# Square roots for the recurrence's rows in three parts inside attention, rows normalized in place and stored in groups, turned blocks copied out on two engines

## The chip, the cores and the metric

The kernel runs on one core of one Trainium2 chip. The metric is the device time of one launch in microseconds (us). Three runs of the kernel before took 3347.38, 3348.98 and 3350.77 us, with a median of 3348.98 us. The core has five engines that run their own instruction queues side by side: TensorE (PE) for matrix products and transposes, VectorE (DVE), ScalarE (ACT), GpSimd (POOL) and SyncE (SP). They meet only through semaphores. Transfers between memory and the core's buffers run on 16 DMA engines. They are issued from the queues of SP, ACT or POOL.

## The reference

Two layers work on `x` (32 batches of 100 rows of 256 numbers) with a context of 361 rows per batch:

```python
x = x + tanh(g_xattn[0]) * L0_xattn(layernorm(x), ctx, ctx, Wq, bq, Wk, bk, Wv, bv, Wo, bo)
x = x + tanh(g_ffn[0])   * L0_ffn(layernorm(x), gru_w_ih, gru_w_hh, expr_w, ctx_w, ctx_b, gate_w, up_w, down_w, ...)
x = x + tanh(g_xattn[1]) * L1_xattn(ctx, layernorm(x))
x = x + tanh(g_ffn[1])   * L1_ffn(layernorm(x), router_w, w1, b1, w2, b2)
```

`L0_xattn` is attention with 16 heads. `L0_ffn` is a GRU of 100 steps that routes rows to experts. `L1_xattn` is an alignment by dynamic programming, and `L1_ffn` a mixture with a capacity. `layernorm(x)` is `(x - mean) / sqrt(var + 1e-5)` over each row. The change touches what lies between attention and the GRU: the normalization of the rows that attention gives.

## The kernel before

The kernel is a chain of stages. Each stage is a block: all five engines run their part, and at its end they meet. Each engine reports to POOL that it has drained (the gather), and POOL releases all of them into the next stage. The stages that matter here are these.

**Attention** (`attention`, about 30 to 750 us of the span) handles one batch in a turn. The 32 turns are software pipelined over the engines: `pipelined` (L218 to L227) writes out turn 0 and turn 31 and puts turns 1 to 30 in a loop of two turns each. In a turn the engines walk over the 16 heads. PE computes the scores of four heads at a time (L573), DVE takes the maxima (L456), ACT the exponentials (L380), PE transposes the results (L581), and DVE and ACT copy the transposed results of even and odd heads out of PSUM (L505, L390). The four score banks are refilled only when the exponentials of the four heads before are done. The output of batch b is projected and added to its row during turn b+1 (L470, L476), its mean and variance go into `mean_var` (L477 to L488), and POOL stores its rows to memory (`store`, L351). At the end POOL waits until all these stores have landed (the wait on `stored`) before it drains.

**Normalized rows out** (`normalized_rows_out`, L123 to L201) is the next stage, about 756 to 786 us. ACT issues the loads of `wc`, `cb` and `gate`, and POOL that of `wih` (3 MB, for the GRU). Then DVE adds the epsilon for all 32 batches at once, ACT takes the square root, and DVE the reciprocal. For every batch DVE normalizes the rows into one of 8 buffers `h` (L163), SP stores this buffer to `h_store` (L144), PE transposes its two halves into one of 8 PSUM banks (L176), and ACT copies the two halves into `hT` and sums each row on the way (L197). DVE may refill a buffer only when its store has landed and its transposes are done. At the end PE multiplies the sums by `wc` (L182), and DVE makes the first state of the GRU from it (L166).

**The GRU** (`gru`) starts at about 786 us. POOL copies its first inputs from `hT`, and PE needs `wih` and `whh`.

The order on each engine is written out by hand. No scheduler moves instructions. An ACT function that needs another table than the one loaded gets an `ACT_TABLE_LOAD` ahead of it. The compiler puts it in.

## Time and profile before

| | us |
|---|---|
| median of three runs | 3348.98 |
| the profiled execution | 3356.15 |
| its span, first to last instruction | 3354.5 |
| attention ends on DVE (mean and variance of batch 31 kept) | 750.55 |
| next stage released | 755.8 |
| GRU released | 785.8 |

| engine | busy us | share |
|---|---|---|
| PE | 2969.9 | 89% |
| DVE | 1424.3 | 42% |
| ACT | 958.9 | 29% |
| POOL | 815.3 | 24% |

Times in the rows below are counted from the start of the span. A row of the timeline that stands for several instructions gives the start of the first, the time until the end of the last and their number. Since an engine overlaps the end of one instruction with the start of the next, the spacing of starts is what one more instruction costs.

### The profile page before, as it was taken

The numbers are of one execution on the slowest core, as the hardware profiler recorded it, in microseconds if no ns is written. First come the engines' busy times: TensorE is split into PE (matmuls) and PEld (weight loads), VectorE is DVE, ScalarE is ACT, GpSimd is POOL, SyncE is SP. The second block draws the span as 40 slices with busy tenths as digits, with TensorE's granted clock in tenths as the row PEclk, the third lists the DMA queues.
The fourth block names the chain that finished last, engine by engine and source line by source line (L and its number), as shares of the span: only waits on it lengthen the run. The fifth ranks groups of instructions, "written<-read, shape, count | busy, mean of one in ns | idle before, by whom it ended". The sixth has DMA issues, their size and how long they took to land. (4 is left out here: it accounts for less than half of the span.)

```text
span 3354.5 us, 72380 instructions
## 1 busy us (share of the span) xinstructions
PE 2969.9 (89%) x27712; PEld 1662.2 (50%) x27713; DVE 1424.3 (42%) x3167; ACT 958.9 (29%) x2643; POOL 815.3 (24%) x771
## 2 busy tenths in 40 slices
PE   5999999988999999999999999999999976008698
PEld 3666666653444444444444444458666644007454
DVE  4666666652222233333323333345222246985311
ACT  2555555543111111111111111122122236472111
POOL 1111001100222222232222222233444422004243
PEclk9999999987999999999999999999999988558699
DMA  6000000003000000000000000041222253005143
GB/s 225 24 21 20 21 23 23 23 11 128 23 16 23 17 23 17 23 17 17 22 17 23 17 23 17 23 176 53 43 45 45 45 148 119 0 0 198 46 115 72
DMA packets 81216, 163.02 MB, mean 49 GB/s; under 512 B 12056, under 2 KB 54936, under 8 KB 76408
## 3 DMA queue, kind: packets, MB, share of 16 engines
q1 hardware_dynamic: 55848, 102.34, 9.7%
q0 software_dynamic: 21504, 40.67, 5.5%
q10 hardware_dynamic: 3664, 17.04, 1.4%
q8 instruction: 162, 2.65, 0.3%
q14 instruction: 38, 0.31, 0.0%
HBM read 119.63 MB, written 40.37 MB: 48 GB/s over the span
## 5 line engine op out<-in xcount | busy, mean ns | idle before, releaser
L926 PE MATMUL gru_ps_rz<-whh,scratch 128*32 128x512 f32 x6400 | 707.4, 594 | 0.0
L734 POOL TENSOR_TENSOR scratch<-scratch 128x1024 f32<-128x1024 f32 (+3 forms) x246 | 369.6, 1527 | 818.5 <-DVE stat L748 657.6
L926 PEld LDWEIGHTS gru_ps_rz<-whh,scratch 128*32 128x32 f32 x6400 | 197.7, 110 | 452.1 <-issue 452.1
L931 PE MATMUL gru_ps_n<-whh,scratch 128*32 128x256 f32 x6400 | 363.6, 379 | 0.0
L855 DVE TENSOR_TENSOR scratch<-scratch,state 128x256 f32<-128x256 f32 x100 | 50.8, 508 | 661.1 <-ACT scratch L884 661.1
L931 PEld LDWEIGHTS gru_ps_n<-whh,scratch 128*32 128x32 f32 x6400 | 207.9, 110 | 180.1 <-issue 59.8
L380 ACT ACTIVATE att_probs<-att_score,att_neg_max 100x361 f32<-100x361 f32 x512 | 260.6, 568 | 122.2 <-DVE att_neg_max L456 122.1
L581 PEld LDWEIGHTS att_turned<-ident,att_probs 100*121 100x121 f32 x1536 | 210.3, 185 | 140.3 <-issue 105.9
L581 PE MATMUL att_turned<-ident,att_probs 100*121 100x100 f32 x1536 | 267.3, 287 | 11.8 <-ACT att_probs L380 5.0
L456 DVE TENSOR_REDUCE att_neg_max<-att_score 100x1 f32<-100x361 f32 x512 | 250.1, 525 | 56.0 <-PE att_score L573 56.0
L884 ACT ACTIVATE scratch<-gru_ps_rz 128x512 f32<-128x512 f32 x100 | 59.7, 597 | 720.3 <-PE gru_ps_rz L926 720.3
L903 PE MATMUL gru_ps_rz<-wih,scratch 128*32 128x512 f32 x1600 | 191.5, 596 | 2.2 <-POOL scratch L823 2.2
L2219 PE MATMUL e_ps_g<-align_reach,ident 32*121 32x101 f32 x64 | 10.9, 326 | 196.8 <-DVE align_reach L2031 195.3
L748 DVE TENSOR_REDUCE stat<-scratch 128x2048 f32 (+3 forms) x96 | 181.1, 1886 | 0.0
L505 DVE COPY att_probsT<-att_turned 121x300 f32<-121x300 f32 x256 | 119.0, 465 | 134.3 <-PE att_turned L581 134.1
L887 ACT ACTIVATE scratch<-scratch 128x256 f32<-128x256 f32 x100 | 41.7, 417 | 349.0 <-DVE scratch L859 349.0
L390 ACT COPY att_probsT<-att_turned 121x300 f32<-121x300 f32 x256 | 103.5, 404 | 131.9 <-PE att_turned L581 131.9
L857 DVE TENSOR_TENSOR scratch<-scratch,gru_ps_n 128x256 f32<-128x256 f32 x100 | 42.1, 421 | 231.7 <-PE gru_ps_n L931 231.7
L573 PE MATMUL att_score<-att_kT,att_qT 32*100 32x361 f32 x1024 | 112.3, 508 | 16.1 <-ACT att_probs L380 15.4
L356 POOL TENSOR_TENSOR att_qT<-att_q_all,att_head_mask 128x400 f32<-128x400 f32 x32 | 27.3, 853 | 379.8 <-DVE att_q_all L444 379.7
L1470 DVE COPY mix_room<-mix_ps_m 128x512 f32<-128x512 f32 x57 | 39.4, 691 | 187.7 <-PE mix_ps_m L1559 187.7
L1147 POOL DMA_INDIRECT x<-mix_room,mix_rows_listed x57 | 90.4, 1586 | 92.1 <-ACT mix_room L1205 87.6
(377 smaller groups left out, 4385.2 us busy)
## 6 DMA issues: line engine op xcount, KB each, us to landing
table<-in_w SPq DMA_DIRECT2D x16, 1024.0 KB, 7.0
states<-state SPq DMA_DIRECT2D x100, 128.0 KB
scratch<-states SPq DMA_DIRECT2D x25, 512.0 KB, 3.6
whh<-in_whhT POOLq DMA_DIRECT2D x8, 1536.0 KB, 17.3
att_c_in<-in_ctxT SPq DMA_DIRECT2D x32, 363.0 KB, 3.0
dist_ctx<-in_ctxT SPq DMA_DIRECT2D x32, 363.0 KB, 5.5
align_ctx<-in_ctx_rows SPq DMA_DIRECT2D x32, 363.0 KB
whh<-in_guT ACTq DMA_DIRECT2D x8, 1024.0 KB, 12.1
```

The costliest lines, as they stand in the source:

```text
L380: nc.scalar.activation(probs[h % KEPT][:, 0:KV], score[h % BANKS][0:S, 0:KV], ACT.Exp, bias=neg_max[:, h % KEPT:h % KEPT + 1], scale=-1.0) ...
L390: nc.scalar.copy(probsT[h // 4 % 2][:, h % 4, :], turned[1][0:KC, 0:3 * S]).then_inc(odd_ready, 1)
L456: nc.vector.tensor_reduce(neg_max[:, h % KEPT:h % KEPT + 1], score[h % BANKS][0:S, 0:KV], AX.X, ALU.min).then_inc(max_ready, 1)
L505: nc.vector.tensor_copy(probsT[h // 4 % 2][:, h % 4, :], turned[0][0:KC, 0:3 * S]).then_inc(even_ready, 1)
L573: nc.tensor.matmul(score[r][0:S, 0:KV], qT[u][strip, half, g, :], kT[u][strip, g, 0:KV], start=True, stop=True).then_inc(s_psum, 1)
L581: done = nc.tensor.transpose(turned[h % 2][0:KC, m * S:(m + 1) * S], probs[h % KEPT][:, m * KC:(m + 1) * KC], ident[0:S, 0:S])
L734: done = nc.gpsimd.tensor_tensor(last.prod[:, row:row + rows, :], a, b, ALU.mult)
L748: nc.vector.tensor_reduce(stat[:, bass.ds(it, 1), at:at + rows].rearrange("p a n -> p (a n)"), last.prod[:, 0:rows, :], AX.X, ALU.add).the ...
L903: nc.tensor.matmul(ps_rz[quarter(q), :], xt[u][:, k, j, :], rz_columns(wih, k, q), start=(k == 0), stop=False)
L926: last = nc.tensor.matmul(ps_rz[quarter(q), :], stateT[c % 2][:, quarter(c // 2)], rz_columns(whh, c, q), start=False, stop=(c == GC - 1))
L931: last = nc.tensor.matmul(ps_n[quarter(q), 0:GQ], stateT[c % 2][:, quarter(c // 2)], n_columns(whh, c, q), start=(c == 0), stop=(c == GC - 1))
L1147: nc.gpsimd.indirect_dma_start(x2, bass.IndirectOffsetOnAxis(ap=rows_listed[:, n:n + 1], axis=0), y[u], None, compute_op=ALU.add).then_inc ...
```

## The change

The roots move into attention. The statistics of batches 0 to 23 are complete when turn 25 runs. In turn 25 DVE adds the epsilon for these 24, ACT takes their root between two attention functions, and in turn 26 DVE inverts them. From turn 26 on, DVE normalizes four of these batches a turn, in place in `rows`, after heads 2, 5, 8 and 11. SP stores them in three groups of eight batches, 800 KB each. After the last turn come the epsilon, root, reciprocal and normalization of batches 24 to 30, around the output of batch 31. Batch 31 itself gets its root in the next stage. For this, the turns from 25 to 31 are written out on ACT and DVE (`pipelined_to`), while PE and POOL keep their loop.

In the next stage PE transposes straight from `rows`, with no normalization ahead of it except for batch 31. Of every 8 batches ACT copies out 5, with its sums, and DVE 3, each with a reduction for the sums and a copy for both halves. The last group of eight batches goes out as one store of 800 KB from SP. SP also issues the loads of `wc`, `cb` and `gate`, which ACT issued before. POOL no longer waits for its stores at the end of attention. DVE does before it writes `rows` in place.

```diff
-            v.tensor_scalar(rstd[:], mean_var[:, :, 1], LN_EPS, None, ALU.add).then_inc(eps_added, 1)
+            v.tensor_scalar(rstd[:, LAST:B], mean_var[:, LAST:B, 1], LN_EPS, None, ALU.add).then_inc(eps_added, 1)
             dve.wait_ge(root_ready, 1)
-            v.reciprocal(rstd[:], rstd[:]).then_inc(scaled, 1)
-            dve.wait_ge(scaled, 1)
+            v.reciprocal(rstd[:, LAST:B], rstd[:, LAST:B]).then_inc(inverted, 1)
             for b in range(B):
-                if b >= RING:
-                    dve.wait_ge(h_stored[b % RING], 16 * (b // RING))
-                    dve.wait_ge(h_turned, b - RING + 1)
-                v.tensor_scalar(h[b % RING][:], rows[:, b, :], mean_var[:, b, 0:1], rstd[:, b:b + 1], ALU.subtract, ALU.mult).then_inc(h_ready, 1)
+                if b == BANKS:
+                    dve.wait_ge(inverted, 1)
+                    for u in range(2):
+                        dve.wait_ge(x1_stored[u], 16 * (B // 2))
+                    v.tensor_scalar(rows[:, LAST, :], rows[:, LAST, :], mean_var[:, LAST, 0:1], rstd[:, LAST:B],
+                                    ALU.subtract, ALU.mult).then_inc(last_ready, 1)
+                if not BY_ACT[b % BANKS]:
+                    dve.wait_ge(h_turned, b + 1)
+                    halves = turned[b % BANKS][:, 0:KT * S].rearrange("p (k s) -> p k s", k=KT)
+                    v.tensor_reduce(x_sum[:, :, b], halves, AX.X, ALU.add).then_inc(sums_done, 1)
+                    v.tensor_copy(hT[:, :, :, b], halves).then_inc(dve_copied, 1)
...
         @block.sync
         def _(sp):
-            for b in range(B):
-                sp.wait_ge(h_ready, b + 1)
-                sp.dma_start(h_rows[b], h[b % RING][:]).then_inc(h_stored[b % RING], 16)
-            for u in range(RING):
-                sp.wait_ge(h_stored[u], 16 * (B // RING))
+            sp.dma_start(wc[:], wcT).then_inc(wc_in, 16)
+            for q in range(4):
+                sp.dma_start(cb[32 * q:32 * q + 32, :], ctx_b[q * GQ:(q + 1) * GQ].partition_broadcast(32)).then_inc(cb_in, 16)
+            sp.dma_start(gate[:, :], g_ffn.partition_broadcast(P)).then_inc(gate_in, 16)
+            sp.wait_ge(last_ready, 1)
+            sp.dma_start(h_rows[:, EARLY:B, :], rows[:, EARLY:B, :]).then_inc(h_stored, 16)
+            sp.wait_ge(h_stored, 16 * (EARLY // 8 + 1))
...
+def pipelined_to(engine, looped, count, turn_of):
+
+    turn_of(0, 0, True, False)
+    with engine.Fori(1, looped // 2 + 1) as i:
+        turn_of(2 * i - 1, 1, False, False)
+        turn_of(2 * i, 0, False, False)
+    for b in range(looped + 1, count):
+        turn_of(b, b % 2, False, b == count - 1)
...
+                    if isinstance(b, int) and b == EARLY + 1 and h == ROOTS:
+                        roots(0, EARLY, 1)
...
-            pipelined(act, B, turn_of)
+            pipelined_to(act, EARLY, B, turn_of)
+            roots(EARLY, B - 1, 2)
             att_out(B - 1)
             attnT_out(B - 1)
...
+                    if isinstance(b, int) and b >= EARLY + 2 and h % 3 == 2 and h < 12 and 4 * (b - EARLY - 2) + h // 3 < EARLY:
+                        normalize_output(4 * (b - EARLY - 2) + h // 3, 1, 16 * (EARLY // 2 + 1), 16 * (EARLY // 2))
...
             pipelined(pool, B, turn_of)
-            store(B - 1)
-            pool.wait_ge(stored, 16 * B)
-            pool.wait_ge(cleared_rows, 16)
+            store(B - 1, 1)
```

Here `EARLY` is 24, `ROOTS` is 6 and `BY_ACT` is `(True, True, False, True, False, True, True, False)`.

ACT in turn 25, from the exponentials ahead of head 6 on. Before, the turn is in the loop (line 378 and 227 rows are register work of the loop, 380 exponentials, 390 the copies of odd heads, 394 and 402 copies of two small transposed blocks):

```order
L380 ACTIVATE att_probs<-att_score,att_neg_max 100x361 [waits att_t_psum,att_max_ready]
L390 COPY att_probsT<-att_turned 121x300 [waits att_o_psum,att_t_psum]
L393 REGISTER_ALU
L394 COPY att_xnT<-att_misc 128x200 [waits att_xnT_psum]
L402 COPY att_attnT<-att_misc 128x200 [waits att_attnT_psum]
L390 COPY att_probsT<-att_turned 121x300 [waits att_o_psum,att_t_psum]
L378 REGISTER_ALU
L227 REGISTER_ALU [waits att_max_ready]
L380 ACTIVATE att_probs<-att_score,att_neg_max 100x361 [waits att_t_psum]
```

The same place in the changed kernel, where 413 are the exponentials, 423 the copies of odd heads, and 440 the root:

```order
L413 ACTIVATE att_probs<-att_score,att_neg_max 100x361 [waits att_t_psum,att_max_ready] x4
L423 COPY att_probsT<-att_turned 121x300 [waits att_o_psum,att_t_psum]
L427 COPY att_xnT<-att_misc 128x200 [waits att_xnT_psum]
L435 COPY att_attnT<-att_misc 128x200 [waits att_attnT_psum]
L440 ACT_TABLE_LOAD
L440 ACTIVATE rstd_x<-rstd_x 100x24 [waits att_eps_added]
L423 COPY att_probsT<-att_turned 121x300 [waits att_o_psum,att_t_psum]
L413 ACT_TABLE_LOAD [waits att_t_psum]
L413 ACTIVATE att_probs<-att_score,att_neg_max 100x361 [waits att_max_ready]
L413 ACTIVATE att_probs<-att_score,att_neg_max 100x361 [waits att_t_psum,att_max_ready] x3
```

Two table loads and the root have come between the copy of the attention output and the next exponential, with the copy of head 7 between the loads.

DVE in turn 26, from the copy of head 2 on. Before (505 copies, 456 maxima, 462 and 464 the division of the batch before):

```order
L505 COPY att_probsT<-att_turned 121x300 [waits att_o_psum,att_t_psum]
L454 REGISTER_ALU
L227 REGISTER_ALU [waits att_s_psum]
L456 TENSOR_REDUCE att_neg_max<-att_score 100x1 [waits att_p_ready]
L454 REGISTER_ALU
L227 REGISTER_ALU [waits att_s_psum]
L456 TENSOR_REDUCE att_neg_max<-att_score 100x1 [waits att_p_ready]
L454 REGISTER_ALU
L227 REGISTER_ALU [waits att_s_psum]
L456 TENSOR_REDUCE att_neg_max<-att_score 100x1 [waits att_p_ready]
L462 RECIPROCAL att_inverse<-att_misc 100x16 [waits att_back_psum]
L464 TENSOR_TENSOR att_attn<-att_misc,att_inverse 100x256 [waits att_inverse_ready]
```

Now (564 copies, 497 maxima, 546 a normalization in place):

```order
L564 COPY att_probsT<-att_turned 121x300 [waits att_o_psum,att_t_psum]
L497 TENSOR_REDUCE att_neg_max<-att_score 100x1 [waits att_p_ready,att_s_psum]
L546 TENSOR_SCALAR rows_x<-rows_x,mean_var,rstd_x 100x256 [waits x1_stored1,x1_stored0,att_rstd_ready]
L497 TENSOR_REDUCE att_neg_max<-att_score 100x1 [waits att_p_ready,att_s_psum] x2
L503 RECIPROCAL att_inverse<-att_misc 100x16 [waits att_back_psum]
L505 TENSOR_TENSOR att_attn<-att_misc,att_inverse 100x256 [waits att_inverse_ready]
L564 COPY att_probsT<-att_turned 121x300 [waits att_o_psum,att_t_psum]
L497 TENSOR_REDUCE att_neg_max<-att_score 100x1 [waits att_p_ready,att_s_psum]
L546 TENSOR_SCALAR rows_x<-rows_x,mean_var,rstd_x 100x256 [waits x1_stored1,x1_stored0,att_rstd_ready]
```

The first normalization of the turn stands between the first and the second of three maxima. The second stands after the maximum of head 7. The register work of the loop is gone.

SP from the end of attention to the GRU. In the changed kernel it issues three grouped stores in attention, then (from L145 on, the next stage) the loads and the last group:

```order
L365 DMA h_store<-rows_x 100x2048 [waits att_h_ready] x3
L284 UNCONDITIONAL_BRANCH
L145 UNCONDITIONAL_BRANCH [waits barrier_Pool_Activation_PE_DVE_SP_release]
L147 DMA wc<-in_wcT 128x2048
L149 DMA cb<-in_ctx_b 32x256 x4
L150 DMA gate_ffn<-in_g_ffn 128x2
L152 DMA h_store<-rows_x 100x2048 [waits last_h_ready]
L129 UNCONDITIONAL_BRANCH [waits h_stored]
```

Before, SP had only the 32 stores of one batch each in that stage. The loads of `wc`, `cb` and `gate` now stand ahead of the last store in SP's own queue.

## Rows read from the trace of the kernel before

**Rows 1.** The page's busy times of the whole span.

```profile
PE 2969.9 (89%) x27712; PEld 1662.2 (50%) x27713; DVE 1424.3 (42%) x3167; ACT 958.9 (29%) x2643; POOL 815.3 (24%) x771
```

**Rows 2.** Windows: us, busy of PE, PEld, DVE, ACT, POOL, then clock, DMA share, GB/s.

```profile
702.00:724.00 22.00, 21.06 (x221) 15.10 (x219) 14.57 (x38) 13.09 (x31) 2.16 (x3) 1.00 0.02 5
724.00:746.00 22.00, 17.52 (x174) 12.16 (x175) 11.15 (x28) 9.57 (x23) 0.54 (x1) 0.75 0.02 5
766.00:768.00 2.00, 0.00 (x0) 0.00 (x0) 0.00 (x0) 0.00 (x0) 0.00 (x0) 0.50 1.15 412
774.00:776.00 2.00, 2.00 (x10) 1.16 (x8) 1.74 (x6) 2.00 (x21) 0.00 (x0) 0.50 0.68 236
```

**Rows 3.** Queue instructions at attention's end (L253): duration ns min/median/max, start.

```profile
L253 POOLq DRAIN  x1: 3407/3407/3407, 752.2 to 752.2; - x1
L253 SPq EVENT_SEMAPHORE  x1: 17/17/17, 755.8 to 755.8; - x1
```

**Rows 4.** The same at the end of the stage after it (L126).

```profile
L126 POOLq DRAIN  x1: 13105/13105/13105, 756.4 to 756.4; - x1
L126 SPq EVENT_SEMAPHORE  x1: 17/17/17, 785.8 to 785.8; - x1
```

**Rows 5.** Timeline of DVE, 740 to 795 us: start, us, what, idle before.

```profile
750.32 0.23 DVE L488 TENSOR_SCALAR mean_var<-att_mean_var_now 100x2 f32<-100x2 f32 x1
...
760.92 2.67 DVE L163 TENSOR_SCALAR h<-rows_x,mean_var,rstd_h 100x256 f32<-100x256 f32 x8
769.83 5.20 DVE L163 TENSOR_SCALAR h<-rows_x,mean_var,rstd_h 100x256 f32<-100x256 f32 x12 [6.24 <-DMA h_store<-h]
...
791.19 0.29 DVE L849 COPY scratch<-gru_ps_t 128x128 f32<-128x128 f32 x1 [5.82 <-PE gru_ps_t L912]
```

**Rows 6.** Timeline of ACT in the stage, 756 to 782 us.

```profile
758.98 1.28 ACT L193 ACT_TABLE_LOAD   x1 [12.24 <-issue]
760.27 0.23 ACT L193 ACTIVATE rstd_h<-rstd_h 100x32 f32<-100x32 f32 x1
...
770.93 0.35 ACT L197 ACTIVATE hT<-turned 128x100 f32<-128x100 f32 x1 [5.05 <-PE turned L176]
...
781.58 0.71 ACT L197 ACTIVATE hT<-turned 128x100 f32<-128x100 f32 x1
```

**Rows 7.** Timeline of PE in the stage.

```profile
761.39 2.93 PE L176 MATMUL turned<-ident,h 100*128 100x100 f32 x16 [12.57 <-DVE h L163]
```

**Rows 8.** DMA issues, 735 to 800 us: count, KB each, median us to landing.

```profile
wih<-in_wihT POOLq DMA_DIRECT2D x1, 3072.0 KB, 13.0
...
gate_ffn<-in_g_ffn ACTq DMA_DIRECT2D x1, 1.0 KB, 11.6
```

**Rows 9.** Timeline of ACT, turn 30, heads 5 to 10.

```profile
708.71 0.35 ACT L402 COPY att_attnT<-att_misc 128x200 f32<-128x200 f32 x1
709.76 0.41 ACT L390 COPY att_probsT<-att_turned 121x300 f32<-121x300 f32 x1 [0.70 <-PE att_turned L581]
710.06 1.47 ACT L380 ACTIVATE att_probs<-att_score,att_neg_max 100x361 f32<-100x361 f32 x3
```

**Rows 10.** Timeline of PE, turn 30 (first three rows) and turn 31.

```profile
707.33 0.56 PE L581 MATMUL att_turned<-ident,att_probs 100*121 100x100 f32 x3
708.37 0.87 PE L573 MATMUL att_score<-att_kT,att_qT 32*100 32x361 f32 x8 [0.47 <-ACT att_probs L380]
...
710.76 0.55 PE L581 MATMUL att_turned<-ident,att_probs 100*121 100x100 f32 x3
...
731.26 0.56 PE L581 MATMUL att_turned<-ident,att_probs 100*121 100x100 f32 x3 [0.96 <-ACT att_probs L380]
...
734.37 1.54 PE L573 MATMUL att_score<-att_kT,att_qT 32*100 32x361 f32 x8
```

**Rows 11.** Timeline of DVE, turn 30, heads 2 to 4.

```profile
704.58 1.41 DVE L456 TENSOR_REDUCE att_neg_max<-att_score 100x1 f32<-100x361 f32 x3 [0.39 <-PE att_score L573]
...
706.81 0.47 DVE L505 COPY att_probsT<-att_turned 121x300 f32<-121x300 f32 x1 [0.19 <-PE att_turned L581]
```

More of the change, by code:

```diff
@@ L120, in normalize, with normalized_rows_out @@
     return nc.vector.tensor_scalar(out, rows, mean[:, bass.ds(b, 1)], rstd[:, bass.ds(b, 1)], ALU.subtract, ALU.mult)
-def normalized_rows_out(nc, rows, mean_var, h_rows, hT, ident, wih, wihT, wih_in, wcT, ctx_b, state, gate, g_ffn):
-    RING, BANKS = 8, 8
+def normalized_rows_out(nc, rows, mean_var, rstd, x1_stored, h_rows, h_stored, cleared_rows, hT, ident, wih, wihT, wih_in,
+                        wcT, ctx_b, state, gate, g_ffn):
+    BANKS = 8
+    BY_ACT = (True, True, False, True, False, True, True, False)
+    LAST = B - 1
     with ExitStack() as ctx:
-        h = [ctx.enter_context(nc.sbuf_tensor(f"h{u}", [S, DIM], F32)) for u in range(RING)]
-        rstd = ctx.enter_context(nc.sbuf_tensor("rstd_h", [S, B], F32))
         x_sum = ctx.enter_context(nc.sbuf_tensor("x_sum", [P, KT, B], F32))
@@ L150, in _ @@
             pool.dma_start(wih[:], wihT).then_inc(wih_in, 16)
+            pool.wait_ge(cleared_rows, 16)
         @block.vector
@@ L330, in _ @@
             repeat(sp, B // 2, turn_of)
+            for g in range(EARLY // 8):
+                sp.wait_ge(h_ready, 8 * g + 8)
+                sp.dma_start(h_rows[:, 8 * g:8 * g + 8, :], rows[:, 8 * g:8 * g + 8, :]).then_inc(h_stored, 16)
         @block.gpsimd
@@ L402, in attnT_out, with roots @@
                 nc.scalar.copy(attnT[:].rearrange("p k s -> p (k s)"), misc[:, 256:256 + KT * S]).then_inc(attnT_ready, 1)
+            def roots(first, end, added):
+                act.wait_ge(eps_added, added)
+                nc.scalar.activation(rstd[:, first:end], rstd[:, first:end], ACT.Sqrt).then_inc(root_ready, 1)
             act.wait_ge(weights_in, 9 * 16)
@@ L488, in keep_statistics, with add_eps, invert, normalize_output @@
                 nc.vector.tensor_scalar(mean_var[:, bass.ds(b, 1), :].rearrange("p a n -> p (a n)"), mean_var_now[:], 1.0, None, ALU.mult).then_inc(stats_kept, 1)
+            def add_eps(first, end):
+                dve.wait_ge(stats_kept, end)
+                nc.vector.tensor_scalar(rstd[:, first:end], mean_var[:, first:end, 1], LN_EPS, None, ALU.add).then_inc(eps_added, 1)
+            def invert(first, end, rooted):
+                dve.wait_ge(root_ready, rooted)
+                nc.vector.reciprocal(rstd[:, first:end], rstd[:, first:end]).then_inc(rstd_ready, 1)
+            def normalize_output(b, inverted, stored_even, stored_odd):
+                dve.wait_ge(rstd_ready, inverted)
+                dve.wait_ge(stored[0], stored_even)
+                dve.wait_ge(stored[1], stored_odd)
+                nc.vector.tensor_scalar(rows[:, b, :], rows[:, b, :], mean_var[:, b, 0:1], rstd[:, b:b + 1],
+                                        ALU.subtract, ALU.mult).then_inc(h_ready, 1)
             normalized(0)
@@ L2504, in build @@
         cleared_rows = ctx.enter_context(nc.semaphore("cleared_rows"))
+        x1_stored = [ctx.enter_context(nc.semaphore(f"x1_stored{u}")) for u in range(2)]
+        h_stored = ctx.enter_context(nc.semaphore("h_stored"))
         weights_in = ctx.enter_context(nc.semaphore("att_weights_in"))
```

70 lines of the change are left out of this document (45 added, 25 removed).

## Prediction

> **What bounds the kernel now.** I read the page's busy times first, then windows around the change, then the queue instructions at the two stage ends, and last the timelines of single engines. PE is busy 89% of the span [rows 1], so a stage without PE is the place to look. In attention PE is busy 21.06 of 22 us at full clock, with DVE and ACT at 14.57 and 13.09 [rows 2]. PE is the bound there, and whatever delays PE is paid in full, since only 0.9 us of a turn is idle. The stage behind it is the reverse. It runs from the release at 755.8 [rows 3] to the release at 785.8 [rows 4], which is 30.0 us, at clock 0.50 [rows 2]. It is paced in turn by ACT's table load, by DVE, which waits 6.24 us for the first store of `h` [rows 5], and by ACT, which starts 48 copies from 770.93 to 781.58, one every 0.227 us [rows 6]. The store that DVE waits for sat behind `wih`: at 766 to 768 the DMA engines are full at 412 GB/s with no engine computing [rows 2], and POOL's drain, which began at 756.4 with `wih`, ends 13.1 us later at 769.5, 0.3 us ahead of DVE's restart [rows 4, 5].
>
> **The end of attention.** DVE is done at 750.55 [rows 5] and the release is at 755.8. In between POOL waits for its last store, then drains for 3.41 us from 752.2 [rows 3]. The change takes the wait away, so the drain starts when POOL has issued its last store, near 750.65. The trace doesn't show what a POOL drain does after small transfers. If it lasts 3.41 us from its own start, it ends at 754.05 and 1.6 us are won. If it needs 3.4 us from the landing, nothing is won. If it ends with the landing at about 752.1, 3.6 us are won. The drain over `wih` lasted 13.1 us, and `wih` landed 13.0 us after its issue [rows 4, 8]: nothing was added behind it, which speaks against the second. I take 1.6, bounds 0 and 3.6.
>
> **The stage behind it** can now be ended by three things, each counted from its release R.
> - Compute. PE starts at about R+0.4. 32 batches of two transposes cost 0.168 us each at clock 0.50 (16 in 2.93 us, less the 0.4 us of the last) [rows 7], so 10.7 us. ACT's share is 20 batches by 0.453, 9.1 us, beside it. DVE's share is 12 by two operations of about 0.3 us, for which the nearest row is the 0.29 us copy out of PSUM [rows 5], 7.2 us. The last batch is DVE's: 0.4 us after PE, then 0.7. That is R+12.2. From ACT's last copy, which ends at 782.3 (781.58 and 0.71) [rows 6], to the release at 785.8 the products, the state and the meeting took 3.5 us. They stay: R+15.7. `wc`, 1 MB ahead of `wih` at some 400 GB/s, is there long before.
> - `wih`. The same 3 MB, issued by POOL at the same place: before, the drain ended 13.7 us after the release [rows 3, 4], so R+13.9 with the release.
> - The last store. It holds 8 batches, 819 kB, and SP waits for its landing. It is ready at about R+5, after eight batches. But it stands in SP's queue behind `wc`, `cb` and `gate`, and `gate` landed 11.6 us after its issue [rows 8], together with `wih`, at 770. I let it start at R+13.2. Stores of 100 partitions ran at 236 GB/s with a DMA share of 0.68 [rows 2], so it takes 3.4 us, and 0.4 more for landing and release: R+17.0. Bounds: 15 if it slips in beside `wih`, 18 if it waits for all of `gate`.
>
> The last is the latest. The stage goes from 30.0 to 17.0 us, a gain of 13.0, bounds 12.0 and 15.9.
>
> The Trainium skill, in "DMA: Bandwidth & Descriptors", section "Queues, rings and completion order", says that each DMA engine takes turns between the queues that have work, packet by packet, and starts the descriptors of one queue in order. Taken as equal shares, the first half would let the last store run beside `wih` from R+6 and land at about R+14. The trace speaks against equal shares: DVE's first store waited until `wih` was over [rows 5]. The second half says that the store can't begin before `gate`, which is what the sum takes.
>
> **What attention pays.** The batches' work is moved under PE, which has no room.
> - The early root (turn 25). ACT ends its small copy at 709.06 in the like place of turn 30 and has 0.70 us until head 7's copy. The exponential of head 8 starts there at 710.06 [rows 9], and PE needs it at 710.76 [rows 10]. A load costs 1.28 and the root 0.23 [rows 6]. So the root ends at 710.6, the copy follows, the second load ends at 712.3, and the exponential is there at 712.85: PE stalls 2.1 us. Bounds: 1.5 (with the copy hiding more) and 2.8 (both loads and the root).
> - Clock. In turn 31 PE idled 0.96 us for an exponential, and the next group of scores took 1.54 us where that of turn 30 took 0.87 [rows 10]; the clock of the window was 0.75 on average [rows 2]. A stall of 2.1 us may do the same in turn 25. The excess is 0.67 us in the scores of four heads, which are a fifth or less of PE's work on them, so a fall that lasts for one group costs about 3.3. I give it 6 in 10, for half of that or all: 1.5, bounds 0 and 3.3.
> - 24 normalizations at 0.33 us (2.67 for 8) [rows 5], four a turn in turns 26 to 31. After head 2 the operation stands between maxima that DVE runs back to back until 705.99, and delays its copy at 706.81, which PE's next transposes into the same bank at 707.33 need [rows 10, 11]. With 0.05 us to spare, 0.28 of 0.33 is paid. After heads 5 and 8 DVE idles, and nothing is paid. After head 11 I take half, 0.17. That makes 0.45 a turn, 2.7 us. Bounds: 0, since the written-out turns also lose the loop's register work, and 8.0 if all is paid.
> - Around the last turn: the reciprocal of 24 in turn 26 and ACT's load and root ahead of the last attention copy. ACT is idle there for most of the 1.5 us. I take 0.5, bounds 0.2 and 1.5. The seven last normalizations lie beside PE's work on batch 31.
>
> The grouped stores of attention meet a DMA share of 0.02 [rows 2] and cost nothing. The sum of costs is 2.1 + 1.5 + 2.7 + 0.5 = 6.8 us.
>
> **Sum.** −1.6 −13.0 +6.8 = −7.8 us. The profiled execution would go from 3356.15 to 3348.4. The median of the runs lies 7.2 us lower than it and moves alike: 3348.98 − 7.8 = 3341.2 us. What a measurement can tell here is about 0.2%, 6.7 us, so the forecast stands just beyond it.
>
> **The rivals.**
> - A. Attention absorbs the work: the clock holds in turn 25, and the shorter queue work of the written-out turns pays for the normalizations. Costs are then 2 to 3 us instead of 6.8, the gain 11 to 13, the time 3337. For it speaks that DVE and ACT are busy only two thirds of a turn [rows 2]; against it, that their order is fixed and the places near head 2 have no idle time.
> - B. The last store isn't last. It slips in beside `wih`, and compute ends the stage at R+15.7, or earlier if the clock rises. Gain 1.6 + 14.3 − 6.8 = 9.1, time 3340; with a risen clock PE is no longer the pace, ACT's 9.1 us are, and R+14.1 gives 3338. Against the rise: with PE busy 2.00 of 2 us on these transposes, the clock stayed 0.50 [rows 2]. The Trainium skill's "TensorE: Matmul & The Clock Gate", on the PE-mode transpose, says that transposes don't count as activity for the full clock. The trace agrees in that window.
> - C. The gain is mostly given back. The clock falls for a full stretch (3.3), the normalizations cost 0.7 a turn (4.2), the root 2.5, and the drain wins nothing: 13.0 − 10.5 = 2.5, time 3346.5.
> - D. Slower. The stalls after head 2 bring the clock down in each of the six turns 26 to 31, as in turn 31 now, at 3.3 us each in five turns more. That is 16.5 us, and the time is 3358. The point from which it decides is a third fall. Against it: PE's idle of 0.9 us a turn left the clock at 1.00 [rows 2], and 0.45 more is half of what turn 31 shows.
>
> **Chances.** The forecast (gain 5 to 10) 0.40, A 0.20, B 0.12, C 0.22, D 0.06. The forecast's gain lies beyond 6.7 us in about 0.24 of its 0.40. With A and B that makes faster 0.56; same is 0.16 + 0.22 and a part of D, 0.40; slower 0.04. The range leaves out D, the lower end of C's band and A's best: 3334 to 3348.
>
> **What would show it.** The drain of POOL at attention's end starts at DVE's end and not 1.5 us later, and lasts 3.4 us. The release of the GRU comes within 0.5 us of SP's last store landing, about 17 us after the stage's own. PE shows one gap of 2 us in turn 25, before the transposes of head 8, and the clock's share there tells whether it fell. DVE's operation after head 2 comes with a PE wait of about 0.3 us in turns 26 to 31. The last statistics end 5 to 9 us later than 750.55. The prediction is wrong if they end before 753, if the stage is shorter than 15 us or longer than 19, or if anything from the GRU on changes its length by more than 1 us.

## The result and the profile after

The changed kernel took 3343.08 us (median of 14 runs, 3335.61 to 3344.52), the kernel before 3350.49 us beside it (14 runs). The ratio is 0.9975, 95% interval 0.9968 to 0.9982: 8.4 us faster, between 6.0 and 10.7 (the two medians alone are 7.4 apart). The forecast was 7.8. A second set of eight runs gave 0.9971 (0.9961 to 0.9981).

The profiled execution took 3336.77 us, 19.4 less than that of before, which is more than the change gives. So the stages come first. The page's top of the changed kernel, beside [rows 1]:

```profile
span 3335.2 us, 72041 instructions
PE 2958.1 (89%) x27712; PEld 1657.6 (50%) x27713; DVE 1432.6 (43%) x3195; ACT 956.5 (29%) x2599; POOL 814.1 (24%) x771
```

The queue instructions at the end of attention (now L284) and of the stage behind it (L129), the answer to [rows 3, 4]:

```profile
L284 POOLq DRAIN  x1: 3994/3994/3994, 748.9 to 748.9; - x1
L284 SPq EVENT_SEMAPHORE  x1: 17/17/17, 753.0 to 753.0; - x1
...
L129 POOLq DRAIN  x1: 13532/13532/13532, 753.7 to 753.7; - x1
L129 SPq COMPARE_BRANCH  x1: 38/38/38, 769.5 to 769.5; - x1
L129 SPq EVENT_SEMAPHORE  x1: 17/17/17, 769.8 to 769.8; - x1
```

The stage behind attention went from 30.0 to 16.8 us (753.03 to 769.85), and SP is the last to arrive, at 769.5: it waited for its store. That is the forecast's 17.0, ended by what it named. The windows in it (us from the span's start, length, busy of PE, PEld, DVE, ACT, POOL, clock, DMA share, GB/s), beside [rows 2]:

```profile
754.00:756.00 2.00, 2.00 (x14) 2.00 (x13) 1.47 (x4) 1.92 (x17) 0.17 (x1) 0.50 0.92 266
758.00:760.00 2.00, 2.00 (x17) 2.00 (x16) 1.64 (x6) 1.92 (x18) 0.00 (x0) 0.62 0.98 410
762.00:764.00 2.00, 0.27 (x4) 0.11 (x4) 1.57 (x5) 1.98 (x19) 0.00 (x0) 1.00 1.14 397
767.00:769.00 2.00, 0.00 (x0) 0.00 (x0) 0.42 (x1) 0.20 (x1) 0.00 (x0) 0.50 0.58 246
```

The DMA engines are full until about 764, and the last store then runs alone, at 246 GB/s and a DMA share of 0.58, about ten of the 16 engines. PE in it (timeline: start, us, what, idle before), the answer to [rows 7]:

```profile
753.15 9.11 PE L195 MATMUL turned<-ident,rows_x 100*128 100x100 f32 x64 [5.48 <-PEq L284]
763.99 1.09 PE L203 MATMUL turned<-wc,x_sum 128*32 128x256 f32 x16 [1.73 <-ACT hT L215]
770.69 1.93 PE L974 MATMUL gru_ps_rz<-wih,scratch 128*32 128x512 f32 x8 [5.61 <-POOL scratch L894]
```

And DVE's last instruction in it:

```profile
767.36 0.42 DVE L180 SCALAR_TENSOR_TENSOR state<-turned,cb 128x256 f32<-128x256 f32 x1 [3.80 <-DMA cb<-in_ctx_b]
```

Two things here weren't in the forecast's sum (R is again the stage's release). The clock rose to 1.00 at 759.5, while PE did nothing but these transposes, so PE's last product was done near R+12. And the state still had to wait for `cb`, to R+14.3: the last 1 KB packets of `cb` moved at R+13.7, beside the end of `wih`.

Attention itself. ACT in turn 25, beside [rows 9]:

```profile
595.96 1.28 ACT L440 ACT_TABLE_LOAD   x1
597.25 0.22 ACT L440 ACTIVATE rstd_x<-rstd_x 100x24 f32<-100x24 f32 x1
597.38 0.39 ACT L423 COPY att_probsT<-att_turned 121x300 f32<-121x300 f32 x1
597.79 1.28 ACT L413 ACT_TABLE_LOAD   x1
599.09 1.47 ACT L413 ACTIVATE att_probs<-att_score,att_neg_max 100x361 f32<-100x361 f32 x3
```

PE in the same turn, beside [rows 10]:

```profile
599.78 0.93 PE L652 MATMUL att_turned<-ident,att_probs 100*121 100x100 f32 x3 [2.28 <-ACT att_probs L413]
600.63 1.23 PE L664 MATMUL att_outs<-att_probsT,att_v 121*32 121x100 f32 x24
...
602.52 2.67 PE L619 MATMUL att_misc<-att_c_in,att_wk 128*128 128x363 f32 x4
```

PE stalls 2.28 us where 2.1 was forecast, and the clock falls: the keys' product takes 2.67 us, where the same four instructions take 1.41 at full clock (at 51.87 us of this profile). The turn is 26.6 us long. Then the end of attention, DVE first, beside [rows 5]:

```profile
740.70 0.20 DVE L539 RECIPROCAL rstd_x<-rstd_x 100x7 f32<-100x7 f32 x1 [2.17 <-ACT rstd_x L440]
743.06 0.90 DVE L546 TENSOR_SCALAR rows_x<-rows_x,mean_var,rstd_x 100x256 f32<-100x256 f32 x2 [2.16 <-DMA x<-rows_x]
743.87 0.25 DVE L503 RECIPROCAL att_inverse<-att_misc 100x16 f32<-100x16 f32 x1
...
749.17 0.23 DVE L529 TENSOR_SCALAR mean_var<-att_mean_var_now 100x2 f32<-100x2 f32 x1
```

PE there:

```profile
741.10 0.64 PE L671 MATMUL att_misc<-ident,att_att 128*100 128x128 f32 x4 [1.08 <-ACT att_att L431]
744.63 0.60 PE L677 MATMUL att_misc<-ident,att_attn 100*128 100x100 f32 x2 [2.89 <-DVE att_attn L505]
```

The same place before:

```profile
745.78 0.60 PE L606 MATMUL att_misc<-ident,att_attn 100*128 100x100 f32 x2 [0.81 <-DVE att_attn L464]
```

DVE waits 2.16 us for the store of batch 30 to land, since the wait ahead of batches 24 and 25 asks for all stores of even batches, and the last batch's division stands behind these two. PE idles 2.89 us for the division, where it idled 0.81 before. The wait is stricter than it need be: what must have landed before batch 24 is written in place is its own store, six batches earlier. No run asked for less.

The stages of all profiles, in us. Attention goes from its release to the next. A turn goes from one write of `xn` (the normalized input of a batch, one a turn) to the next, the last turn from the last `xn` to the last statistics. Low is how long the clock stood at 0.50 within it and rose again; a further fall, 5.6 to 10.8 us ahead of the last statistics, comes in every profile, lasts into the next stage and isn't counted. Exit goes from the last statistics to the release.

| kernel | attention | stage | root's turn (low) | last turn (low) | exit |
|---|---|---|---|---|---|
| before | 725.3 | 29.98 | 21.45 (0) | 48.6 (6.8) | 5.3 |
| changed | 722.8 | 16.82 | 26.6 (6.8) | 47.9 (0) | 3.6 |
| changed, again | 727.7 | 16.79 | 27.0 (6.8) | 47.9 (0) | 3.6 |
| root as Copy | 725.1 | 16.84 | 21.7 (0) | 50.8 (6.8) | 3.6 |
| normalized twice | 733.7 | 16.90 | 25.4 (3.4) | 51.9 (6.8) | 3.6 |
| division first | 721.6 | 16.92 | 23.8 (0) | 49.2 (6.8) | 3.6 |
| loads on ACT | 729.1 | 17.21 | 25.4 (3.4) | 50.8 (6.8) | 3.6 |
| store sooner | 730.2 | 15.26 | 25.4 (3.4) | 50.8 (6.8) | 4.6 |
| root on DVE | 726.3 | 17.66 | 22.8 (0) | 50.9 (10.2) | 3.6 |
| wait back | 728.8 | 16.85 | 26.8 (6.8) | 47.9 (0) | 5.3 |
| last by SP | 724.0 | 16.97 | 26.8 (6.8) | 48.4 (0) | 0.4 |
| best, ACT root | 722.7 | 18.85 | 25.4 (3.4) | 49.5 (6.8) | 0.4 |
| best | 718.3 | 19.30 | 22.8 (0) | 49.1 (6.8) | 0.4 |
| no fourth | 719.5 | 16.76 | 22.8 (0) | 47.8 (3.4) | 0.4 |

Attention's length also holds its first two turns. They took 47.8 us before and 42.5 in the first profile of the changed kernel, where the clock's first record at 1.00 is at 46.1 us instead of 59.3. In the other profiles they took 42.6 to 48.1, with no tie to the code. 5.3 of the 19.4 us are that, and 4.9 came from unchanged stages behind the GRU.

### The profile page after: what moved, and what is told of

Read it like the earlier page. It is cut to its first block and busy times, and to the rows that moved or that the text cites. A ratio compares the mean times of both kernels' runs of the same rounds, so it can differ in the third digit from the quotient of the medians.

```text
span 3335.2 us, 72041 instructions
## 1 busy us (share of the span) xinstructions
PE 2958.1 (89%) x27712; PEld 1657.6 (50%) x27713; DVE 1432.6 (43%) x3195; ACT 956.5 (29%) x2599; POOL 814.1 (24%) x771
## 6 DMA issues: line engine op xcount, KB each, us to landing
whh<-in_guT ACTq DMA_DIRECT2D x8, 1024.0 KB, 12.4
```

## The experiments

All have 5 timed rounds; ratios are to the kernel before. A single kernel's interval is 3 to 5 us to either side, so no two of these ratios tell a term of 1 to 3 us apart. For such terms the profiles' stages decide, one profile for each kernel.

**The changed kernel again** (no edit).

> The changed kernel again, unaltered, as the yardstick of this set: ratio to before 0.9975 (-8.4 us). What its profile should repeat, if my reading of the first trace is of the kernel and not of that execution: the turn with the early root about 5 us longer than its neighbours (26.6 against 21.5), the stage behind attention 16.8 us long, ended by the last store. What should scatter: the first turns (22 to 26 us, by the moment at which the granted clock first rises) and a fall of the clock in the last turn of attention (there or not, 3.3 us). The rival, that these two are effects of the change, wants them as in the first trace: the early rise, and no fall in the last turn.

3340.5 us, 0.9971 (0.9961 to 0.9981). The root's turn was 27.0, the stage 16.79, and the exit 3.62. The first two turns took 46.9 us (47.8 in the kernel before): the early rise was not the change's. But the fall in the last turn stayed away again. That part of the rival held.

**The early root as a Copy.**

```diff
-nc.scalar.activation(rstd[:, first:end], rstd[:, first:end], ACT.Sqrt)
+nc.scalar.activation(rstd[:, first:end], rstd[:, first:end], ACT.Sqrt if added == 2 else ACT.Copy)
```

It leaves out the root of batches 0 to 23, so their rows come out wrongly scaled.

> The early root's instruction on ScalarE becomes a Copy of the same 24 columns (no root is taken of them, so the rows of batches 0 to 23 in the recurrence's input are scaled wrongly): the instruction, its semaphores and everything behind it stay, only the two table loads of 1.28 us go. Theory: the 5.1 us by which that turn is longer are the two loads (2.3 us in which TensorE waits for the exponentials) and the fall of the granted clock they set off (6.8 us at 0.50, some 3 us): the turn comes down to 21.4 to 21.8, no fall in it, ratio to before 0.9960 (0.9953 to 0.9966). Rival 1 (the bounds of my prediction): the stall alone costs, the clock falls anyway: -2.1, ratio 0.9969, and the fall stays. Rival 2: the turn is long because the loop ends there and its code goes on straight: turn stays at 26.6, ratio 0.9975.

3339.5 us, 0.9970 (0.9959 to 0.9980). The turn fell from 27.0 to 21.7 as the theory said, but attention only from 727.7 to 725.1. The clock, in the turn with the root and in the last turn (windows as above):

```profile
590.00:612.00 22.00, 21.07 (x220) 15.06 (x218) 15.14 (x40) 13.11 (x32) 2.16 (x3) 1.00 0.07 23
722.00:746.00 24.00, 16.81 (x176) 11.46 (x174) 13.49 (x37) 11.32 (x25) 0.54 (x1) 0.80 0.13 39
```

The same windows of the changed kernel, run again:

```profile
590.00:612.00 22.00, 18.92 (x166) 13.04 (x167) 10.91 (x27) 13.06 (x27) 1.45 (x2) 0.84 0.07 22
722.00:746.00 24.00, 19.79 (x241) 13.64 (x230) 17.67 (x48) 14.39 (x32) 1.85 (x3) 0.96 0.14 42
```

Without the loads the fall of 6.8 us is back in the last turn, where the kernel before has it too. So the root costs its stall, and the fall only changes place: the root's turn and the last turn together are 74.9 us with the root and 72.5 without, 2.5 us for the root. The expected 5 was wrong. The rival that the written-out code makes the turn long is out: the turn is 0.2 us above the 21.45 of before.

**Each normalization twice.**

```diff
+if b < EARLY:
+    nc.vector.tensor_scalar(spare[:], rows[:, b, :], mean_var[:, b, 0:1], rstd[:, b:b + 1], ALU.subtract, ALU.mult)
 nc.vector.tensor_scalar(rows[:, b, :], ...)
```

> Each of the 24 normalizations inside attention is done twice, once more into a spare tile. My prediction put each at 0.11 us of delay to TensorE (0.45 us a turn, 2.7 us for six turns, bounds 0 and 8.0); in the changed kernel's trace the six turns with them are as long as those without. Theory now: VectorE has 5 us free in a turn of 21.5, a single 0.34 us instruction between two maxima is hidden by the ring of kept probabilities: turns 26 to 31 stay within 0.1 us each, total +0.3 (0 to 1), ratio 0.9975 to 0.9978. Rival (the prediction's term): +0.45 us a turn and more, since two in a row are 0.68 us: +2.7 to +5, ratio 0.9983 to 0.9990. Rival 2 (the prediction's case D): VectorE's delays make TensorE wait often enough that the clock falls in these turns: +15 us, ratio 1.002.

3344.61 us, 0.9987 (0.9978 to 0.9996). Turns 26 to 29 took 21.42, 21.55, 21.63 and 21.56 us in both profiles of the changed kernel (21.45 and 21.56 in turn before), and 22.16, 22.16, 22.23 and 22.15 here. Four single normalizations cost 0.04 us a turn or nothing. Doubled, they cost 0.63 a turn more: the slack at these places is one instruction deep. That is the rival's size; the expected +0.3 us was meant for a DVE with more room. DVE, turn 27, heads 2 and 5:

```profile
643.54 0.41 DVE L549 TENSOR_SCALAR att_spare<-rows_x,mean_var,rstd_x 100x256 f32<-100x256 f32 x1
643.86 0.41 DVE L550 TENSOR_SCALAR rows_x<-rows_x,mean_var,rstd_x 100x256 f32<-100x256 f32 x1
644.18 0.97 DVE L498 TENSOR_REDUCE att_neg_max<-att_score 100x1 f32<-100x361 f32 x2
```

**The division first.**

```diff
-for b in range(EARLY, EARLY + 2):
-    normalize_output(b, 2, 16 * (B // 2), 16 * (B // 2 - 1))
 divide(B - 1)
-for b in range(EARLY + 2, B - 1):
+for b in range(EARLY, B - 1):
```

> The last batch's division stands ahead of the normalizations of batches 24 and 25, which wait for the store of batch 30 to land. Theory: in the changed kernel's trace that wait (2.16 us) and the two normalizations held the division back from 741.9 to 743.9, and TensorE idled 2.89 us for it; with the order turned, the division comes 2.0 us earlier, the seven normalizations (0.34 us each, 2.4 us) fit into the gap in which TensorE turns and projects the last batch (3.0 us), attention's end comes 1.7 to 2.0 us earlier: ratio to before 0.9969 to 0.9971. Rival: the normalizations now stand between the division and the last output, and the store's landing decides again: from landing 743.1 plus 7 x 0.34 = 745.5 before the last output can start, which was to start at 745.8; if the store lands 1 us later the gain falls to 1, and below 0.5 if TensorE at a low clock needs the time anyway.

3338.55 us, 0.9971 (0.9960 to 0.9983). The last turn is 49.2 us. It is 50.8 in the three profiles that have the changed kernel's order at the end of attention and the same fall of 6.8 us (root as Copy, loads on ACT, store sooner): 1.6 us won, a little under the 1.7 to 2.0. DVE now (division, seven normalizations, output):

```profile
741.52 0.26 DVE L503 RECIPROCAL att_inverse<-att_misc 100x16 f32<-100x16 f32 x1 [1.35 <-PE att_misc L669]
...
742.44 2.35 DVE L546 TENSOR_SCALAR rows_x<-rows_x,mean_var,rstd_x 100x256 f32<-100x256 f32 x7 [0.20 <-DMA x<-rows_x]
745.44 0.48 DVE L511 SCALAR_TENSOR_TENSOR att_x<-att_misc,att_gate,rows_x 100x256 f32<-100x256 f32 x1 [0.65 <-PE att_misc L682]
```

**The small loads back on ACT's queue.**

```diff
-sp.dma_start(wc[:], wcT).then_inc(wc_in, 16)
+act.dma_start(wc[:], wcT).then_inc(wc_in, 16)
...
-sp.dma_start(gate[:, :], g_ffn.partition_broadcast(P)).then_inc(gate_in, 16)
+act.dma_start(gate[:, :], g_ffn.partition_broadcast(P)).then_inc(gate_in, 16)
```

> The loads of wc, cb and gate go back to ScalarE's queue, where the kernel before had them; SyncE's queue holds the last grouped store alone. Nothing else changes. Theory 1 (the way my prediction argued: the store is last because it stands behind cb in its queue): the store starts as it is issued, 4.1 us behind the release instead of 12.5, is over by 10 to 12, and the stage ends with the load of wih or with the state, 14.3 to 15 us long instead of 16.8: -1.8 to -2.5. Theory 2, which I now hold likelier: the DMA engines of this stage are full (busy shares of 0.92 to 1.14 in five slices of 2 us, 5.0 MB to move in the stage), so that whatever the store gains wih and cb lose, above all on the ten engines that carry the store: the stage stays at 16.0 to 16.9 us, only the last one of the transfers changes. Ratio to before 0.9968 to 0.9975; the profile's stage length decides.

3340.58 us, 0.9972 (0.9961 to 0.9982). The stage got no shorter: 17.21 us. The store was issued at R+5.7 and its packets moved from R+9.4, beside `wih`, but the last one ended at R+16.0, where it is R+16.2 in the changed kernel. So its place in the queue alone didn't hold it up. The second theory held, that the engines had no room for it before. What ended the stage is neither's: `gate`, now beside the store, was through at R+16.0 too, and ACT took its tanh last.

```profile
776.21 0.20 ACT L218 ACTIVATE gate_ffn<-gate_ffn 128x2 f32<-128x2 f32 x1 [2.58 <-DMA gate_ffn<-in_g_ffn]
L129 SPq COMPARE_BRANCH  x1: 38/38/38, 776.0 to 776.0; - x1
L129 ACTq COMPARE_BRANCH  x1: 43/43/43, 776.4 to 776.4; - x1
```

**A fourth group, stored inside attention.**

```diff
+sp.wait_ge(h_ready, B - 1)
+sp.dma_start(h_rows[:, EARLY:B - 1, :], rows[:, EARLY:B - 1, :])
...
-sp.dma_start(h_rows[:, EARLY:B, :], rows[:, EARLY:B, :])
+sp.dma_start(h_rows[:, LAST:B, :], rows[:, LAST:B, :])
```

> Batches 24 to 30, normalized by the end of attention, are stored from there in a fourth group, and only batch 31 is left for the stage behind. Theory: 0.70 MB (3.0 us of ten engines at 236 GB/s) leave the stage in which the engines are full and go to the last 3 to 5 us of attention, where they are idle; the stage ends with the load of wih (13.5 us after its issue in the changed kernel's trace, now 0.5 to 1 sooner) or with the state, which waits for cb: 14.2 to 15.0 us instead of 16.8: -1.8 to -2.6; attention's end stays, or the small stores of batch 31 land later behind the group and the drain with them (+0 to +1). Ratio 0.9963 to 0.9970. Rival: the group runs on into the next stage and takes the same engines from wih there: the stage stays above 16.

3340.85 us, 0.9973 (0.9962 to 0.9984). The stage is 15.26 us (-1.5, where 1.8 to 2.6 were expected), and POOL's drain before it is 5.00 (+1.0). Together they give 0.5. The stage is now ended by the state's wait for `cb`:

```profile
773.50 0.42 DVE L180 SCALAR_TENSOR_TENSOR state<-turned,cb 128x256 f32<-128x256 f32 x1 [4.49 <-DMA cb<-in_ctx_b]
```

**The early root on DVE.**

```diff
+nc.vector.tensor_scalar(yi, x.bitcast(I32), 1, None, ALU.logical_shift_right)
+nc.vector.tensor_scalar(yi, yi, -1.0, float(0x5f3759df), ALU.mult, ALU.add)
...
+nc.vector.scalar_tensor_tensor(t, y, -0.5, y, ALU.mult, ALU.mult)
+nc.vector.tensor_tensor(t, t, x, ALU.mult)
+nc.vector.scalar_tensor_tensor(y, t, 1.5, y, ALU.add, ALU.mult)
...
-roots(0, EARLY, 1)
```

> The early root (24 columns) leaves ScalarE: VectorE forms the inverse root itself, by a first guess from the bits and three Newton steps, 11 small instructions (0.16 to 0.2 us each, two for one root and reciprocal before), one at each head of turn 25 from head 6 on. No table load in that turn. Theory: the turn falls from 26.6 or 27.0 us (23.8 where the clock did not fall) to 21.5 to 21.9, as with the Copy in its place (21.67), the added 1.9 us of VectorE lie in its free time. But the clock's fall only moves: in the four kernels run so far in which it did not fall in the root's turn, or no root was there, it fell for 6.8 us in the last turn (some 3.3 us), so the gain is 2.3 (the stall) and not 5: ratio 0.9964 (0.9958 to 0.9972). Rival 1: the fall in the last turn is not tied to it and the whole 5 us come: 0.9956. Rival 2: VectorE's added instructions lengthen the turn as the doubled normalizations did (+0.6 a turn): gain 1.7.

3338.58 us, 0.9965 (0.9951 to 0.9978). The turn was 22.8 and not the Copy's 21.7, and the next one 21.16 instead of 21.42: the eleven instructions cost 0.9, which the expectation had put at nothing. The fall in the last turn came as expected, and lasted 10.2 us. Root's and last turn together are 73.7, 1.2 less than with ACT's root. The stage was 17.66 us here, since the store's last packet ended at R+17.0 and not at R+16.2. `wc`, first in that queue, had been through at R+5.5 and not at R+4.5. What held it is not known.

**The wait back.**

```diff
 store(B - 1, 1)
+for u in range(2):
+    pool.wait_ge(stored[u], 16 * (B // 2))
```

> POOL waits again for the landing of all its stores before it goes to the end of attention, as in the kernel before; nothing else. Theory: the drain starts at the landing of the last store (about 2 us behind its issue) instead of at the issue, and lasts 3.4 us as before instead of 4.0: from VectorE's last instruction to the release 5.2 instead of 3.6 us: +1.6, ratio to before 0.9976 to 0.9980. Rival 1: the drain takes the store's flight in anyway: +0.3 or less. Rival 2: the whole flight is added to a drain of 4.0 us: +2.2.

3341.58 us, 0.9975 (0.9965 to 0.9986). The exit went from 3.62 to 5.34 us, the drain from 3.99 back to 3.41:

```profile
L284 POOLq DRAIN  x1: 3407/3407/3407, 754.5 to 754.5; - x1
L284 SPq EVENT_SEMAPHORE  x1: 17/17/17, 758.1 to 758.1; - x1
```

The term is 1.7 us by the exits. The ratio (0.9975 beside 0.9971) is too coarse for it and doesn't contradict it.

**The last two stores from SP.**

```diff
-if not first:
+if not first and not last:
     store(b - 1, 1 - u)
...
-store(B - 1, 1)
...
+sp.wait_ge(x1_kept, B - 2 + 1)
+sp.dma_start(x_rows[:, B - 2, :], rows[:, B - 2, :]).then_inc(stored[2], 16)
+sp.wait_ge(x1_kept, B - 1 + 1)
+sp.dma_start(x_rows[:, B - 1, :], rows[:, B - 1, :]).then_inc(stored[3], 16)
```

> The attention's output rows of the last two batches are stored from SyncE's queue and not POOL's, so that POOL's last DMA is issued a turn (21 us) before the end of attention. Theory: the 4.0 us between POOL's last issue and the release (the DRAIN row of 3994 ns, 5.0 us with the fourth group in flight, 3.4 when the store had landed before it began) are paid because POOL issued a DMA shortly before; with none it takes a few tenths of a us, as POOL's other drains without a DMA (0.05 to 0.26 us), and the release follows VectorE's last instruction by 0.3 to 0.6 us instead of 3.6: -3.1 to -3.4, ratio 0.9961 to 0.9965. Rival 1: the drain's time is POOL's whatever it did 20 us ago (its share of a queue that was used in the block): it stays at 3.4 or more, gain 0 to 0.6. Rival 2: SyncE's own end waits for its stores to land, 2 us behind their issue: gain 1.5. All three see the seven late normalizations start 0.5 to 1.5 us sooner, if a store from SyncE lands sooner than one from POOL (2.0 against 3.7 us).

3338.48 us, 0.9969 (0.9957 to 0.9981). The exit is 0.42 us, 3.2 less. The ratio, 0.9969 beside 0.9971, doesn't resolve it:

```profile
L283 POOLq DRAIN  x1: 4449/4449/4449, 722.0 to 722.0; - x1
L283 SPq DRAIN  x1: 218/218/218, 751.8 to 751.8; - x1
L283 SPq EVENT_SEMAPHORE  x1: 17/17/17, 752.5 to 752.5; - x1
```

The gain came, but not as I had put it. POOL's drain isn't short; it is as long as ever (4.45 us). It begins 30 us ahead of the end, where nobody waits. SP's drain takes 0.22 us and doesn't wait for its stores: the last one's packets moved until 0.4 us behind the release.

**All together**, with the early root on ACT and on DVE. Two edits more than above: `cb` and `gate` are loaded inside attention, and ACT's copy comes ahead of the late root.

```diff
 repeat(sp, B // 2, turn_of)
+small_loads(sp)
...
-roots(EARLY, B - 1, 2)
 att_out(B - 1)
+roots(EARLY, B - 1, 2)
```

> Everything that the runs so far point to, with the early root left on ScalarE: last two stores from SyncE; batches 24 to 30 stored in a fourth group inside attention; cb and the gate loaded by SyncE inside attention; the division ahead of the late normalizations; ScalarE copies the last outputs before it takes the late root. Sum over the stages, against the changed kernel: drain -3.1 to -3.4; order at the end -1.6 (measured by itself, 50.55 to 48.93 us from the last turn's start to VectorE's end) and up to -1.2 more for the copy ahead of the table load; stage behind 16.8 to 14.0 to 14.5 (the load of wih is last, 13.5 us from its issue at 0.5): -2.3 to -2.8. Together -8 to -9 us: 3331 to 3333 at the medians of these sets, ratio 0.9943 to 0.9951. Rival: the gains do not add, since the fourth group and the last store share the engines with the next stage's loads (the stage's engines are full): drain and stage give back 2, ratio 0.9952 to 0.9958.

> As the one before, and the early root on VectorE. Against it: the root's turn 22.8 instead of 23.8 (no fall of the clock in it), 25.4 (a fall of 3.4 us) or 26.6 to 27.0 (6.8 us), and with it a fall in the last turn (2.9 us), which came in all runs but those with the fall of 6.8 in the root's turn: -1.0 to -2.6, ratio 0.9937 to 0.9948. Rival: nothing, as the clock takes back what the table loads cost (then the two agree within 1 us).

3336.79 us, 0.9963 (0.9950 to 0.9977), and 3334.28 us, 0.9955 (0.9941 to 0.9969). The two differ by 2.5 us, inside the expected 1.0 to 2.6 but within the noise. Both miss their expected ratios. Attention behaved, the stage did not: 18.85 and 19.30 us instead of 14 to 14.5. PE in the second:

```profile
751.67 6.39 PE L190 MATMUL turned<-ident,rows_x 100*128 100x100 f32 x50
765.52 1.96 PE L198 MATMUL turned<-wc,x_sum 128*32 128x256 f32 x16 [7.46 <-DMA wc<-in_wcT]
```

`wc` was late. Packets of the fourth group moved until 752.5 (the release was 749.2), so `wc`, behind it in SP's queue, began only at 753.2. `wih` was under way by then, and the two went one packet for one.

**Without the fourth group**, all else of the second kept.

> The best of these versions without the fourth group: batches 24 to 31 are stored together behind attention again, as in the changed kernel; all else of it stays (last two stores from SyncE, cb and gate loaded inside attention, early root on VectorE, division ahead of the late normalizations, copy ahead of the table load). Theory: in the best version the fourth group (0.70 MB, in flight from 747 to 752) held wc back in SyncE's queue until POOL's load of wih had begun (751), from then on one packet of 8 KB of wc went for one of 24 KB of wih, wc landed at 764, and the state and with it the stage ended at R+19.3. Without the group wc starts 1 us behind the release, alone on the engines for 2.5 us as in the changed kernel, and the grouped store runs beside wih: the stage ends with both at R+15.5 to R+16.9, so 2.4 to 3.8 us come back; the rest of attention stays: ratio 0.9943 to 0.9951. Rival (the order of the queue has no part, the stage moves the same bytes either way): R+18 to R+19.3, ratio 0.9955.

3332.3 us (five runs, 3328.71 to 3335.17), 0.9949 (0.9936 to 0.9963), the fastest version. The stage is 16.76, 2.5 us back, at the long end of the expected 15.5 to 16.9. `cb` no longer holds the state, and the store ends the stage again:

```profile
L129 POOLq DRAIN  x1: 14567/14567/14567, 748.5 to 748.5; - x1
L129 SPq COMPARE_BRANCH  x1: 38/38/38, 764.2 to 764.2; - x1
L129 SPq EVENT_SEMAPHORE  x1: 17/17/17, 764.5 to 764.5; - x1
```

## Why the prediction was right

The sum came out within 1 us of the ratio (7.8 against 8.4), partly by errors that cancel. By its steps:

- **The stage behind attention, -13.0.** Right in size and in what ends it: 30.0 to 16.8 us, -13.2, in every profile with this stage 16.8 to 17.7. The store's first packet moves as `gate` gets through, 12.4 us behind the release (13.2 forecast), the last one ends 3.4 to 3.7 later, and 0.6 more pass to the release. The reason given, its place in the queue, was half of it. With the queue cleared the store ended no sooner (R+16.0), and with `cb` and `gate` gone neither (R+16.1); with 0.7 MB less to move, the stage fell to 15.3. It moves 5.0 MB (`wih` 3.1, `wc` 1.0, the store 0.8). That these bytes fill the engines which carry the store is the reading that fits all three; how full each single engine was, the profile doesn't tell.
- **The compute in it, R+15.7.** Too late by about 3: the clock rose to 1.00 at R+6.5 under back-to-back transposes. The forecast had argued against that from a window of the kernel before with PE "busy 2.00 of 2 us" [rows 2]. Records of transposes overlap, so that share hides gaps: the window holds 10 of them, the one from 754 here 14 at the same clock. The rise did not matter, because the store was last. The Trainium skill's "TensorE: Matmul & The Clock Gate", on PE-mode transposes, says that the full clock doesn't engage for them; here PE did nothing else from 753.15 to 759.5, and the clock rose while they ran in all 13 profiles of this stage, 3.9 to 9.3 us behind the release. The measurement decides against the page.
- **The drain, -1.6.** Right: the exit went from 5.3 to 3.6 us, and the wait put back costs 1.7. The drain itself grew from 3.41 to 3.99 us.
- **The early root, 2.1.** Right: PE idles 2.28 us, and where the clock held, the turn is 2.4 us longer (23.8 against 21.45).
- **The clock, 1.5.** In the root's turn it fell for 6.8 us in four profiles with the root on ACT, for 3.4 in four, and not at all in one. The code of that turn is the same in all nine, so the spread isn't the code's. I had left out that the fall in the last turn, which the kernel before pays already, stays away when the root's turn had the whole one. The two then cancel; with a fall of 3.4 it comes on top, at 1.6 (25.4 against 23.8). So 0 to 1.6 net. That they exclude each other is what nine profiles have in common; why is not shown.
- **24 normalizations, 2.7.** The mis-sized term: about 0.2 us in all. The 0.05 us of spare time that I had read behind head 2 was too strict. [rows 11] itself shows DVE idle for 0.19 us ahead of that copy, which the sum left out; the doubled run shows that the slack holds 0.33 us and not 0.67.
- **Around the last turn, 0.5.** The other mis-sized term: 2.2 us (50.8 against 48.6 with the same fall). The step that failed is "the seven last normalizations lie beside PE's work on batch 31": two of them stand ahead of the division and wait for a store. 1.6 of it goes with the order turned; the rest is not taken apart.

What attention pays was forecast as 6.8. It is 2.3 + 0 to 1.6 + 0.2 + 2.2, that is 4.7 to 6.3, and with the stage and the drain the total is -8.6 to -10.2, where the sets measured -8.4 and -9.7. So 2.5 us too much for the normalizations met 1.7 too little at the end: that the sum is this close is partly luck.

Two of the signs that I had set call the forecast wrong in the first profile, and a third, the PE wait of 0.3 us a turn, did not come. The two were badly set. The last statistics (749.4 in the first profile, 754.0 in the second) move with the first turns by 5 us, and the unchanged stages differ by up to 4 us between profiles (312.3 to 316.4 for one of them). The GRU's +1.5 us in the first profile was +0.1 in the second: the clock rose 6.7 us behind its release in the first, 3.8 in the second and 3.9 in the kernel before.

Of the rivals, A put the cost too low (2 to 3 us), and C's and D's did not come. B's risen clock came without its result, as the store was last.

## What to carry to other kernels

When a stage's DMA engines are full, count its bytes before its queues: reordering the small loads moved nothing here, and moving 0.7 MB out of it gave 1.5 us. When the 0.7 MB stood in the queue ahead of the stage's first load, they cost 2.5. A GpSimd queue that issues a DMA shortly before a barrier makes all engines pay for its drain; issue the last ones from another queue (3.2 us here for two small stores). Before pricing an instruction in a bound loop, double it once: one 0.33 us instruction between two others was free, two were not. Where a fall of the clock is part of a price, add up all the places in which it can fall: the fall moved here from one turn to another, and half of the expected gain with it.

## What the runs showed of the hardware

- POOL's drain behind its small stores is 3.4 us if they had landed, 4.0 to 4.5 if it follows the issue, and 5.0 with a 0.7 MB group of another queue in flight. SP's behind its stores is 0.21 to 0.27 us, with packets still moving (last two stores by SP).
- Beside `wih` (packets of 24 KB, 0.93 us each on an engine) a queue of small descriptors advances by one for one. In the changed kernel's second profile, from 763 to 767, 16 to 20 packets of `wih` a us went with 17 to 19 small ones (mostly `cb`'s, 1 KB), and four loads of 32 KB took as long as 3 MB. The Trainium skill's "DMA: Bandwidth & Descriptors", section "Queues, rings and completion order", has the engines take turns between queues packet by packet; the records agree with the turns. By them a turn is one packet of the profile, and it doesn't count bytes. This is also why the kernel before's first stores of `h` landed only as `wih` ended, which the forecast had rightly read as a sign against equal shares: a store of 100 packets of 1 KB goes at the pace of 24 KB packets.
- `wih`'s first packet moves 3.5 to 3.8 us behind POOL's issue in 12 of the 14 profiles (issue at 758.2, first packet at 761.9 in the second of the changed kernel), just as `wc` gets through. In the two profiles where `wc` came late, it moved 1.3 and 1.4 us behind the issue. So the gap isn't a fixed start of POOL's queue, and whether `wih` held back for `wc` isn't shown.
